# ScalarE takes the bounded drops and the adjacency cast, row maxima and copies are regrouped, and the turns of five engines are redrawn

## The chip, the cores and the metric

The kernel runs on one core of one Trainium2 chip. The metric is device time in microseconds (us) from start to end of one launch; lower is better. The core has four compute engines that run their own instruction streams in program order and meet by semaphores: TensorE (PE, with weight loads shown apart as PEld), VectorE (DVE), ScalarE (ACT) and GpSimd (POOL); SyncE (SP) issues the DMAs.

## The reference

`x` is 16 graphs of 512 nodes with 128 features, `adj` 16 adjacency matrices of 512 x 512. Eight residual blocks follow one another, each on a layer norm of `x`, and no graph needs another:

```python
def reference(x, adj, ...):
    x = x + _L0_gnn_ref(_layernorm(x), adj, ...)   # g0: 3 steps of messages and a GRU cell
    x = x + _L0_ffn_ref(_layernorm(x), ...)        # f0: 8 experts, top 2
    x = x + _L1_gnn_ref(_layernorm(x), adj, ...)   # g1: graph attention, masked softmax, elu
    x = x + _L1_ffn_ref(_layernorm(x), ...)        # f1: attention over 64 slices, 8 heads
    x = x + _L2_gnn_ref(_layernorm(x), adj, ...)   # g2: mean of neighbours, relu
    x = x + _L2_ffn_ref(_layernorm(x), ...)        # f2: Mamba2 block, chunks of 128
    x = x + _L3_gnn_ref(_layernorm(x), adj, ...)   # g3: two layers of 4-head masked attention
    x = x + _L3_ffn_ref(_layernorm(x), ...)        # f3: feed-forward on the top half of the rows
    return x
# in f2, the state stage:
#   Lmat = exp(segsum(dA)): exp of A_cum[l] - A_cum[s] where s <= l, 0 elsewhere
#   Y_diag = einsum('bcln,bcsn,bhcls,bcshp->bclhp', Cc, Bc, Lmat, xdt)
# in g1 and g3: softmax over neighbours, exp(score - row maximum)
```

## The kernel before, in words

Each graph goes through an early half (g0, f0, g1, f1) and a late half (g2, f2, g3, f3). The kernel has 17 half-steps: half-step h runs the early half of graph h and, interleaved with it on every engine, the late half of graph h-1. Half-step 0 has only early work, half-step 16 only late work, and the 15 between have both; they are called periods here. Two sets of tiles (lane 0 and 1) alternate.

What each engine does is written as two Python generators, one for the early and one for the late half, each `yield` being the end of a step. The function `halves` draws steps from the two by a string of letters: `e` is one early step, `l` one late step, `p` a step of the next graph's preparation. For TensorE a digit or `w` issues two small bf16 products of a constant identity into a PSUM bank (`keep_bank`, L1060, tile `ident_bf`, and `keep`, L1056): nobody reads them. Called keeps here, they stand where TensorE would otherwise wait. The strings PE_FIRST, DVE_FIRST and so on hold for half-step 0, PE_TURNS, ACT_TURNS, DVE_TURNS, POOL_TURNS and SP_TURNS for the 15 periods, PE_LAST for half-step 16. So the order on an engine is written out by hand, and every wait is a semaphore between steps. Early TensorE work uses PSUM banks 0 to 2, late work banks 3 to 7.

The steps that the change and the prediction touch:

- g2: `g2_adjacency` casts the int32 adjacency (128 x 2048) to fp32 for the message products, on GpSimd, once per graph (L2082).
- f2: TensorE projects and convolves (`f2_gate`, L444), transposes by constant products (`f2_turn`, L756), then `f2_rows` (TensorE, L794) lays the row copies of the cumulated decays into banks 4, 5, 6 and 3, 4 heads x 128 columns each. VectorE's `f2_rows` (L1362, 16 instructions of 128 x 128) forms min(row - column, 0), ScalarE's `f2_decays` takes exp of it in two pieces of 128 x 1024, and VectorE's `f2_weigh` (L1359) multiplies them into the weights that TensorE uses for Y_diag.
- g1: VectorE's `g1_scores` gives masked scores and one maximum per row tile, `g1_max` finishes all four maxima, ScalarE's `g1_leaky` runs 4 times and `g1_exp` 4 times, TensorE turns the result.
- g3: per layer 16 blocks (4 row tiles x 4 heads), each masked (DVE L1860), exponentiated (ACT), normalised (POOL L2089) and transposed by TensorE (`g3_turn`, L903). The transposed block is copied out of PSUM by `g3_turned`: every fourth one by VectorE (L1877), the other three by ScalarE (L1068, tiles adjf and scratch).
- f1: `to_columns` (L453) transposes the normalised rows, then projections, slice softmax, `f1_mix` and `f1_out`, whose end releases the next graph's first product.

Of the kernel before, what the change touches and what calls it, by code (L numbers as in the profile page):

```python
# [20 lines left out]
ALU = mybir.AluOpType  # L21
# [3 lines left out]
P = 128  # L25
# [52 lines left out]
    "lleele"  # L78
)
PE_FIRST = (  # L80
    "eewwwwwweeeeeeeeeewwwwwwwwwwwwwwwwwwwwwwwwwwwwwwwwweeeeeeeeeewwwwwwwwwwwwwwwwwwwwwwwwwwwwwwwwweeeeee"
    "eeeewwwwwwwwwwwwwwwwwwwwwwwwwwwwwwwwweppeeeewwwwwwwwweeeeeeeeeeeeeeeeeeeeeeeeeeeeeeeeeeeeeeeeeeeewww"
    "wwwwwwwweeeeewwwwwwwwwwwwwwwwwwwwwwwwwwwwwwwwwwweeeewwwwwweeewwwwwwwwwwwwwwwwwwwwwwwwwwwwwwwwwwweeww"
    "wwwwwewwwwwewwwwwweeeewwwwwwwwwwwwwwwwwwwwwwwwwwwwwwwwwwweeeewwwwwwewwwwewwwwwwwwwwwwwwwwwwweewwwwwe"
    "wwwwwwwwwwwwwwwwwwwwwwewwwwwwweeeeewwwwwwwwwwwwwwwwwwwwwwwwewwwwwwwewwwwwweewwwwwwwwwwwwewwwwwwewwww"
    "wweeee"
# [3 lines left out]
    "wwwwwwwwwlllwwlwlllllllwwwwwwwwwwwwwwwwwwwwwwwwwwwwwwwwwwwlllllllwwwlwwwwwwwwwwwwwwwwwwwwwwwwwllllww"  # L90
    "wwwwwwwwwwwwwwwwwwwwwwwwwwwwwwwwwllllwwwwwwllllwwwwwwwwwwwwwlwwwwwwwwwwwwwwwwwwwwwwwwwwwwllwwwwwwwww"
    "lwwwwwwwwwwwwlllwwwwwwwlwwwwwwwwlwwwwwwwwwwwwlllwwwwwwllllwwwwlwwwwwwwwlwwwwwwwwwwwwllwwwlwwwwwllwwl"
    "wwwwwwllllwllllwwwwwwwwwwwwwlwwwwwwwwwwwwwwwwwwwwwwwwwwwwllwwwwwwwwwlwwwwwwwwwwwwlllwwwwwwwlwwwwwwww"
    "lwwwwwwwwwwwwlllwwwwwwllllwwwwlwwwwwwwwlwwwwwwwwwwwwllwwwlwwwwwllwwlwwwwwwllllwwwllllwwwwwwwwwwwwwww"
    "wwwwwwwwwwwwwwwwwwwwllllwwwwwwllllwwwwwwwl"
# [8 lines left out]
    "ee7777eelellll7777lllllleeeeeeellll7777lllleleeleeeeeellell7lllllll11eeeeeeeeellellll77l7l7777777777"  # L104
    "7e777777777777lllleeee777777eee777777777lleelleelllleeleeee7777leeelleeeeellleleele33333llllllleeeel"
    "eeeeleeeeeeeeeeell44eellelleellll33lleleeeleee7l7777777777777777777eele77e777777leeeel1111lll11111l1"
    "1111111111l11eeeelellellllel111111lellel44ll4lelllleeeeelllle77777e77777ellllelellelelllelee"
)
ACT_TURNS = (
    "eellleeelellllllleellllleleelellleeeeleeeeeelleelllleelllllllllllllleeelelleeleelllllllleleeeeeeelee"  # L110
    "eelleellllllelllllelllelelelellllllelelleleeeeleellll"
)
DVE_TURNS = (
# [2101 lines left out]
```

## Time and profile before

| | |
|---|---|
| time, median of 3 runs | 3431.71 us (3428.83 to 3431.92) |
| the profiled execution | 3433.32 us, of it the span 3431.5 us |
| TensorE clock granted, mean | 0.994 of full |
| PE busy | 3231.9 us, 94% |
| DVE busy | 2208.7 us, 64% |
| ACT busy | 1752.7 us, 51% |
| POOL busy | 693.3 us, 20% |

The busy share says how long an engine had an instruction in flight. For TensorE it includes the keeps, so 94% is not 94% of needed work. The 17 half-steps can be told apart in the trace by the transposes of `x_in_ln` (L453), which open each early half.

### The profile page before, as it was taken

What the parts mean: (1) busy time and instruction counts of PE and PEld (TensorE: products, weight loads), DVE (VectorE), ACT (ScalarE), POOL (GpSimd) and SP (SyncE); (2) the same over time, 40 slices, a digit from 0 to 9 for tenths busy, and PEclk for the clock granted to TensorE, in tenths of its full rate; (3) what the DMA queues carried; (4) which work ended last, traced back from release to release, by engine and by line L of the source; (5) the groups of instructions that cost most, each with busy time, mean ns of one, the idle gap of its engine ahead of it and who ended that gap; (6) DMA issues with size and microseconds to landing.
All of it is one profiled execution on the core that took longest, in us unless ns stands there. A gap on an engine that the chain in (4) does not pass through costs nothing.

```text
span 3431.5 us, 62674 instructions
## 1 busy us (share of the span) xinstructions
PE 3231.9 (94%) x24744; PEld 2268.1 (66%) x24776; DVE 2208.7 (64%) x7062; ACT 1752.7 (51%) x3195; POOL 693.3 (20%) x804
## 2 busy tenths in 40 slices
PE   8999999999999999999999999999999999999989
PEld 5766666666666666666666666666666666666677
DVE  3476666757567676666757567676666757566653
ACT  2237454563645537454563645537454563645524
POOL 0012122121221212122121221212122121221212
PEclk9999999999999999999999999999999999999999
DMA  3000000000000000000000000000000000000000
GB/s 132 2 7 1 20 4 17 7 1 20 4 17 7 1 22 1 19 4 17 7 1 19 4 17 7 1 22 1 19 4 17 7 1 19 1 4 4 1 8 5
DMA packets 28773, 40.68 MB, mean 12 GB/s; under 512 B 1344, under 2 KB 17728, under 8 KB 28224
## 3 DMA queue, kind: packets, MB, share of 16 engines
q1 hardware_dynamic: 28480, 36.67, 3.4%
q8 instruction: 197, 3.23, 0.4%
q14 instruction: 96, 0.79, 0.1%
HBM read 28.28 MB, written 4.19 MB: 9 GB/s over the span
## 4 chain that ended last, share of the span: by engine, by line
PE 56%; DVE 26%; ACT 11%; issue 5%; POOL 2%; DVEq 0%
PE ps L444 45%; ACT scratch L1068 8%; DVE scratch L1359 5%; PE ps L903 4%; DVE scratch L1362 4%; DVE scratch L1365 3%; DVE scratch L1860 3%; PE ps L453 2%; DVE x L1365 2%; PE ps L1056 2%; DVE stats L1380 2%; POOL rstd L2066 1%; ACT adjf L1068 1%; DVE xn L1362 1%; ACT xT L1068 1%
## 5 line engine op out<-in xcount | busy, mean ns | idle before, releaser
L1068 ACT ACTIVATE scratch<-scratch 128x512 f32<-128x512 f32 (+4 forms) x832 | 564.8, 691 | 278.9 <-DVE scratch L1359 128.9
L444 PE MATMUL ps<-xT,weights_sb 128*128 128x512 f32 x1152 | 560.9, 604 | 7.9 <-ACT xT L1068 7.8
L444 PE MATMUL ps<-scratch 128*128 128x128 f32 (+6 forms) x4608 | 534.4, 379 | 35.7 <-ACT adjf L1068 14.1
L2089 POOL TENSOR_SCALAR scratch<-scratch 128x512 f32<-128x512 f32 x512 | 352.6, 703 | 933.0 <-DVE scratch L1867 932.3
L1068 ACT ACTIVATE scratch<-ps 128x512 f32<-128x512 f32 (+2 forms) x512 | 286.5, 566 | 426.2 <-PE ps L444 230.7
L444 PE MATMUL ps<-weights_sb,scratch 128*128 128x128 f32 (+3 forms) x3840 | 492.6, 278 | 5.9 <-DVE scratch L1503 5.9
L444 PEld LDWEIGHTS ps<-weights_sb,scratch 128*128 128x128 f32 (+3 forms) x3840 | 442.2, 184 | 56.8 <-issue 29.2
L444 PEld LDWEIGHTS ps<-scratch 128*128 128x128 f32 (+5 forms) x4608 | 341.4, 159 | 174.2 <-issue 92.1
L903 PE MATMUL ps<-weights_sb,scratch 128*128 128x128 f32 x2048 | 307.0, 279 | 61.4 <-ACT adjf L1068 24.6
L2066 POOL TENSOR_TENSOR rstd<-ve,minus_half 128x4 f32<-128x4 f32 x126 | 142.9, 1134 | 1081.0 <-DVE ve L1362 1081.0
L1860 DVE CUSTOM_DVE_ANT_0 scratch<-ps,nomask 128x512 f32<-128x512 f32 x512 | 332.7, 683 | 10.5 <-PE ps L444 10.2
L444 PEld LDWEIGHTS ps<-xT,weights_sb 128*128 128x128 f32 x1152 | 197.9, 190 | 212.8 <-issue 145.0
L903 PEld LDWEIGHTS ps<-weights_sb,scratch 128*128 128x128 f32 x2048 | 222.3, 141 | 170.9 <-issue 104.2
L1060 PE MATMUL ps<-ident_bf 128*128 128x128 bf16 x4140 | 300.4, 219 | 0.0
L1068 ACT ACTIVATE scratch<-ps,weights_sb 128x512 f32<-128x512 f32 x368 | 244.8, 686 | 88.5 <-PE ps L444 87.7
L1060 PEld LDWEIGHTS ps<-ident_bf 128*128 128x128 bf16 x4140 | 264.4, 99 | 34.1 <-issue 29.4
L1068 ACT ACTIVATE scratch<-ps,made_sb 128x512 f32<-128x512 f32 x176 | 120.4, 684 | 301.2 <-PE ps L444 301.0
L1068 ACT ACT_TABLE_LOAD x202 | 259.2, 1283 | 18.2 <-PEq L252 14.7
L1068 ACT ACTIVATE xT<-ps 128x512 f32<-128x512 f32 x112 | 66.9, 597 | 342.4 <-PE ps L453 342.4
L444 PE MATMUL ps<-adjf,scratch 128*32 128x256 f32 (+1 forms) x1280 | 241.6, 425 | 0.0
L1365 DVE SCALAR_TENSOR_TENSOR x<-ps,scratch,x 128x128 f32<-128x128 f32 x576 | 161.8, 344 | 111.5 <-PE ps L444 93.6
L1068 ACT ACTIVATE adjf<-ps 128x512 f32<-128x512 f32 (+1 forms) x288 | 166.3, 577 | 89.5 <-PE ps L903 67.2
(166 smaller groups left out, 4520.1 us busy)
## 6 DMA issues: line engine op xcount, KB each, us to landing
adj<-adj SPq DMA_DIRECT2D x16, 1024.0 KB, 5.7
weights_sb<-weights SPq DMA_DIRECT2D x1, 4605.0 KB, 19.0
x_in<-x SPq DMA_DIRECT2D x16, 256.0 KB, 2.8
scratch<-scratch SPq DMA_DIRECT2D x32, 128.0 KB, 2.3
out<-x SPq DMA_DIRECT2D x16, 256.0 KB, 2.4
scratch<-raw SPq DMA_DIRECT2D x1, 1645.0 KB, 22.4
weights_sb<-weights SPq DMA_DIRECT2D x1, 499.0 KB, 6.5
scratch<-raw SPq DMA_DIRECT2D x1, 384.0 KB, 4.9
```

The source lines that it names most:

```text
L444: return pe.matmul(o, lhsT, rhs, start=start, stop=stop, **k)
L453: last = pe.transpose((ep if k < G2 else lp)(0, P, P, t * P), rows[:, t, 0:D], ident)
L903: last = pe.transpose(lp(turn_bank(n), P, P, j * P), probabilities(g, layer, n)[:, tile(j)], ident)
L1056: pe.matmul(ep(0, P) if h else lp(3, P, P, 384), ident_bf[:, :], ident_bf[:, :], start=True, stop=True)
L1060: pe.matmul(banks[k][0:P, 0:P], ident_bf[:, :], ident_bf[:, :], start=True, stop=True)
L1068: return act.activation(o, a, func, **k)
L1359: return v.tensor_tensor(o, a, c, op)
L1362: return v.tensor_scalar(o, a, s1, s2, op0, op1, **k)
L1365: return v.scalar_tensor_tensor(out=o, in0=a, scalar=s1, in1=c, op0=op0, op1=op1, **k)
L1860: v.tensor_tensor_reduce(probabilities(g, layer, n), lp(n % AH), NM[g][:, n // AH, :], -1.0, 4 * BIG, ALU.add, ALU.min, cut(g, G3_MX + n, ...
L2066: pool.tensor_tensor(rstd[g][:, :], ve[g][:, :], minus_half[:, :], ALU.pow).then_inc(s[f"rstd_ready{g % LANES}"], 1)
L2089: pool.tensor_scalar(p, p, cut(g, G3_RI + n, 1), 1.0, ALU.mult, ALU.mult).then_inc(s["att_p"], 1)
```

## The change

It has these parts.

- The bounded drops of f2 leave VectorE. ScalarE's new `f2_drops` forms relu(column - row) with scale -1 and the column as bias, and `f2_decays` takes exp with scale -1. The second `f2_rows` exp of ScalarE now stands after the third group of drops.
- `g2_adjacency` leaves GpSimd for ScalarE (a Copy of 128 x 2048), and stands after the third `g0_candidate`.
- `g1_max` works on pairs of row tiles, with one semaphore step for each pair, and ScalarE's order is leaky 0, leaky 1, exp 0, leaky 2, exp 1, leaky 3 and so on.
- The copies of g3's transposed blocks are split evenly: even blocks on VectorE (16 per graph, before 8), odd ones on ScalarE (16, before 24).
- All turn strings are redrawn. Per period the keeps go from 276 to 290 products, in half-step 0 from 756 to 750 by its string, in half-step 16 from 1034 to 1074.

```diff
 PE_TURNS = (
-    "ee7777eelellll7777lllllleeeeeeellll7777lllleleeleeeeeellell7lllllll11eeeeeeeeellellll77l7l7777777777"
+    "ee7777eeeeelelleleleelllllleeeeeeellll7777llllell7777777777777777777777777777777leellllllllleleeeeel"
...
@@ semaphores @@
-            "... "m1_ready": 1, ...
+            "... "m1_ready": T // 2, ...
-            "... "pT_dve": 2 * T, "pT_act": 2 * T * (AH - 1), ...
+            "... "pT_dve": T * AH, "pT_act": T * AH, ...
         def turned(layer, n, g):
-            if n % AH == 0:
-                return done("pT_dve", g, layer * T + n // AH)
-            return done("pT_act", g, (layer * T + n // AH) * (AH - 1) + n % AH - 1)
+            return done("pT_act" if n % 2 else "pT_dve", g, (layer * T * AH + n) // 2)
@@ ScalarE @@
+                def g2_adjacency(g):
+                    yield
+                    act.wait_ge(*done("aggr_psum", g, GNN0_STEPS - 1))
+                    f(AF[g][:, :, :], ADJ[g][:, :, :], ACT.Copy).then_inc(s["adjf_ready"], 1)
@@
-                    if t == 0:
-                        act.wait_ge(*done("m1_ready", g))
+                    if t % 2 == 0:
+                        act.wait_ge(*done("m1_ready", g, t // 2))
@@
+                def f2_drops(g):
+                    for n, c in enumerate((1, 2, 3, 0)):
+                        yield
+                        act.wait_ge(*done("row_psum", g, n))
+                        for h in range(MH):
+                            a = F2_S + 9 * 16 + c * MH + h
+                            last = f(cut(g, F2_E + (c * MH + h) * P, P), lp(c, P, P, h * P), ACT.Relu, scale=-1.0, bias=SC[g][:, a:a + 1])
+                        last.then_inc(s["dd_ready"], 1)
+                        if n == 2:
+                            yield from f2_rows(g, 1)
@@ f2_decays
-                        f(e, e, ACT.Exp).then_inc(s["e_ready"], 1)
+                        f(e, e, ACT.Exp, scale=-1.0).then_inc(s["e_ready"], 1)
@@ g3 on ScalarE
-                            if n > AH and n % AH:
+                            if n > AH and n % 2:
                                 yield from g3_turned(g, layer, n - AH)
@@ VectorE
-                def f2_rows(g):
-                    for n, c in enumerate((1, 2, 3, 0)):
-                        yield
-                        v.wait_ge(*done("row_psum", g, n))
-                        for h in range(MH):
-                            a = F2_S + 9 * 16 + c * MH + h
-                            last = ts(cut(g, F2_E + (c * MH + h) * P, P), lp(c, P, P, h * P), SC[g][:, a:a + 1], ALU.subtract, 0.0, ALU.min)
-                        last.then_inc(s["dd_ready"], 1)
@@
+                            if q:
+                                yield from g3_turned(g, layer, (q - 1) * AH + 2)
@@ GpSimd
-                def g2_adjacency(g):
-                    yield
-                    pool.wait_ge(*done("aggr_psum", g, GNN0_STEPS - 1))
-                    pool.tensor_copy(AF[g][:, :, :], ADJ[g][:, :, :]).then_inc(s["adjf_ready"], 1)
```

How the instructions stand in a row, at the places of which the prediction speaks. Names: ps0 to ps7 are PSUM banks; in the rows of one period here scratch1, xT1 and adjf1 (or those with 0) belong to one graph and the other number to the other.

ScalarE around the decays of f2 (late graph 0, early graph 1), before:

```order
955 L1068 ACTIVATE scratch1<-ps0,made_sb 128x512
956 L1068 ACTIVATE scratch1<-scratch1,weights_sb 128x512
957 L1068 ACTIVATE adjf0<-ps7 128x512
958 L1068 ACTIVATE scratch1<-ps1 128x512
959 L1068 ACTIVATE adjf0<-ps7 128x256
960 L1068 ACTIVATE scratch0<-scratch0 128x1024 x2
961 L1068 ACTIVATE scratch1<-ps0,made_sb 128x512
```

and with the change:

```order
905 L1066 ACTIVATE scratch1<-ps0,made_sb 128x512
906 L1066 ACTIVATE scratch1<-scratch1,weights_sb 128x512
907 L1066 ACTIVATE adjf0<-ps7 128x512
908 L1066 ACTIVATE scratch0<-ps4,scratch0 128x128 x4
909 L1066 ACTIVATE scratch0<-ps5,scratch0 128x128 x4
910 L1066 ACTIVATE scratch0<-ps6,scratch0 128x128 x4
911 L1066 ACTIVATE adjf0<-ps7 128x256
912 L1066 ACTIVATE scratch0<-ps3,scratch0 128x128 x4
913 L1066 ACTIVATE scratch1<-ps1 128x512
914 L1066 ACTIVATE scratch0<-scratch0 128x1024 x2
```

The 16 drops stand between the two exponentials of the rows, and the early graph's copy (scratch1 from ps1) stands behind all of them.

VectorE at the same place, before:

```order
1820 L1359 TENSOR_TENSOR scratch1<-xT1,scratch1 128x512
1821 L1365 SCALAR_TENSOR_TENSOR scratch1<-scratch1 128x512
1822 L1362 TENSOR_SCALAR scratch0<-ps4,scratch0 128x128 x4
1823 L1365 SCALAR_TENSOR_TENSOR xT1<-scratch1 128x512
1824 L1362 TENSOR_SCALAR scratch0<-ps5,scratch0 128x128 x4
1825 L1362 TENSOR_SCALAR scratch0<-ps6,scratch0 128x128 x4
1826 L1362 TENSOR_SCALAR scratch0<-ps3,scratch0 128x128 x4
1827 L1359 TENSOR_TENSOR scratch0<-adjf0,scratch0 128x768
1828 L1359 TENSOR_TENSOR scratch0<-scratch0 128x768
1829 L1414 COPY scratch1<-ps1 128x512
1830 L1359 TENSOR_TENSOR scratch0<-scratch0 128x1024 x2
```

and with the change:

```order
1862 L1776 COPY scratch0<-ps6 128x512
1863 L1379 TENSOR_TENSOR scratch1<-xT1,scratch1 128x512
1864 L1385 SCALAR_TENSOR_TENSOR scratch1<-scratch1 128x512
1865 L1385 SCALAR_TENSOR_TENSOR xT1<-scratch1 128x512
1866 L1379 TENSOR_TENSOR scratch0<-ps3,weights_sb 128x512
1867 L1379 TENSOR_TENSOR scratch0<-adjf0,scratch0 128x768
1868 L1379 TENSOR_TENSOR scratch0<-scratch0 128x768
1869 L1379 TENSOR_TENSOR scratch0<-scratch0 128x1024
1870 L1434 COPY scratch1<-ps1 128x512
1871 L1379 TENSOR_TENSOR scratch0<-scratch0 128x1024
```

The drops are gone, the early graph's new state (xT1) is no longer between them, and its copy from ps1 stands between the two long products.

TensorE after the projections of f2 (`f2_gate`, the products from xT1), before:

```order
516 L444 MATMUL ps5<-xT1,weights_sb 128x512
517 L444 MATMUL ps1<-adjf0,scratch0 128x512 x3
518 L444 MATMUL ps0<-xT0,weights_sb 128x512
519 L444 MATMUL ps2<-scratch0,made_sb 128x512
520 L444 MATMUL ps1<-scratch0,made_sb 128x512
521 L756 MATMUL ps6<-weights_sb,scratch1 128x128 x4
```

and with the change:

```order
517 L442 MATMUL ps5<-xT1,weights_sb 128x512
518 L1058 MATMUL ps7<-ident_bf 128x128 x62
519 L754 MATMUL ps6<-weights_sb,scratch1 128x128 x4
520 L442 MATMUL ps1<-scratch0,made_sb 128x512
521 L442 MATMUL ps0<-scratch0,made_sb 128x512
522 L754 MATMUL ps4<-weights_sb,scratch1 128x128 x4
```

Between the last projection and the first transpose stood early message and gate products; they now come before the projections, and 62 keeps stand there.

TensorE at the end of a period, from the slice softmax of f1 to the next graph's first transpose, before:

```order
479 L671 MATMUL ps1<-weights_sb,scratch1 64x128 x4
480 L949 MATMUL ps5<-weights_sb,scratch0 128x128 x4
481 L444 MATMUL ps3<-xT0,weights_sb 128x512
482 L444 MATMUL ps0<-scratch1 64x128 x8
483 L444 MATMUL ps4<-xT0,weights_sb 128x512
484 L444 MATMUL ps1<-scratch1 128x128 x4
485 L444 MATMUL ps6<-weights_sb,scratch0 128x128 x12
486 L444 MATMUL ps1<-scratch1 128x128 x4
487 L444 MATMUL ps6<-weights_sb,scratch0 128x128 x4
488 L444 MATMUL ps1<-scratch1 128x128 x8
489 L453 MATMUL ps0<-weights_sb,x_in_ln0 128x128 x4
```

and with the change:

```order
481 L442 MATMUL ps0<-scratch1 64x64 x8
482 L442 MATMUL ps6<-weights_sb,scratch0 128x128 x12
483 L669 MATMUL ps1<-weights_sb,scratch1 64x128 x4
484 L1058 MATMUL ps7<-ident_bf 128x128 x10
485 L442 MATMUL ps0<-scratch1 64x128 x8
486 L442 MATMUL ps6<-weights_sb,scratch0 128x128 x4
487 L442 MATMUL ps1<-scratch1 128x128 x16
488 L451 MATMUL ps0<-weights_sb,x_in_ln0 128x128 x4
```

The late graph's f3 (ps3, ps4, ps6) has moved ahead, and f1's last products (ps1) stand together behind it.

## Rows read from the trace of the kernel before

**Rows 1.** The page: span, and busy time of each engine.

```profile
span 3431.5 us, 62674 instructions
PE 3231.9 (94%) x24744; PEld 2268.1 (66%) x24776; DVE 2208.7 (64%) x7062; ACT 1752.7 (51%) x3195; POOL 693.3 (20%) x804
```

**Rows 2.** Windows of one period in three stretches, and of half-step 16; columns named.

```profile
core 0: us, PE busy (x) PEld busy (x) DVE busy (x) ACT busy (x) POOL busy (x), PEclk, DMA share, GB/s
...
1001.57:1067.19 65.62, 62.75 (x382) 40.27 (x383) 51.23 (x136) 27.21 (x40) 8.58 (x6) 1.00 0.11 29
1067.19:1125.80 58.61, 55.50 (x414) 38.45 (x412) 32.75 (x116) 41.52 (x73) 12.96 (x18) 1.00 0.00 1
1125.80:1207.34 81.54, 76.48 (x658) 56.23 (x657) 53.20 (x190) 41.16 (x87) 21.90 (x26) 1.00 0.00 1
...
3264.00:3431.50 167.50, 151.19 (x1710) 123.36 (x1708) 78.97 (x265) 62.86 (x126) 29.88 (x40) 0.96 0.02 6
```

**Rows 3.** The same three stretches, keeps alone (tile ident_bf: PE, PEld, DVE busy).

```profile
1001.57:1067.19 65.62, 6.05 (x82) 5.46 (x82) 0.00 (x0) 1.00 0.11 29
1067.19:1125.80 58.61, 3.72 (x52) 3.38 (x52) 0.00 (x0) 1.00 0.00 1
1125.80:1207.34 81.54, 10.26 (x142) 8.79 (x142) 0.00 (x0) 1.00 0.00 1
```

**Rows 4.** Timeline of PE: f1's first transpose and the next graph's, half-step 0, then period.

```profile
137.94 1.10 PE L453 MATMUL ps<-weights_sb,xn 128*128 128x128 f32 x4 [2.87 <-DVE xn L1362]
...
177.79 0.60 PE L453 MATMUL ps<-weights_sb,x_in_ln 128*128 128x128 f32 x4
...
1156.51 1.09 PE L453 MATMUL ps<-weights_sb,xn 128*128 128x128 f32 x4 [0.33 <-DVE xn L1362]
...
1207.34 0.66 PE L453 MATMUL ps<-weights_sb,x_in_ln 128*128 128x128 f32 x4 [0.17 <-DVE x L1365]
```

**Rows 5.** Chain that ended last, a piece of f2 in this period.

```profile
1050.42 2.58 DVE scratch L1359 x2
```

**Rows 6.** DVE by form, f2_weigh's long products: period 1001.57 on, then half-step 16.

```profile
L1359 DVE TENSOR_TENSOR scratch<-scratch 128x1024 f32<-128x1024 f32 x2 | 4.3, 2208 | 0.0
...
L1359 DVE TENSOR_TENSOR scratch<-scratch 128x1024 f32<-128x1024 f32 x2 | 2.4, 1222 | 0.0
```

**Rows 7.** Timeline of POOL at the same place of the period.

```profile
1049.63 1.94 POOL L2082 CAST adjf<-adj 128x2048 f32<-128x2048 int32 x1 [30.05 <-PE ps L444]
1051.53 2.06 POOL L2070 TENSOR_TENSOR x<-x,weights_sb 128x512 f32<-128x512 f32 x1
```

**Rows 8.** Timeline of DVE in half-step 16: the 16 drops.

```profile
3304.92 4.22 DVE L1362 TENSOR_SCALAR scratch<-ps,scratch 128x128 f32<-128x128 f32 x16 [2.26 <-PE ps L794]
```

**Rows 9.** Timelines of ACT: short and long instructions of its kinds.

```profile
1046.83 2.00 ACT L1068 ACTIVATE scratch<-scratch 128x1024 f32<-128x1024 f32 x2 [1.51 <-DVE scratch L1362]
...
1107.24 0.38 ACT L1068 ACTIVATE scratch<-ps 128x256 f32<-128x256 f32 x1
1107.51 0.69 ACT L1068 ACTIVATE scratch<-ps,weights_sb 128x512 f32<-128x512 f32 x1
...
3291.08 0.22 ACT L1068 ACTIVATE scratch<-scratch 128x16 f32<-128x16 f32 x1
```

**Rows 10.** g3's copies: DVE by form in the period, ACT in its timeline.

```profile
L1877 DVE COPY scratch<-ps 128x512 f32<-128x512 f32 x8 | 5.5, 690 | 9.7 <-PE ps L903 9.7
...
1099.80 0.57 ACT L1068 ACTIVATE adjf<-ps 128x512 f32<-128x512 f32 x1
```

**Rows 11.** PE's waits in the period: in total, times, longest.

```profile
PE ps L903 <- ACT adjf L1068: 1.6, 5, 0.4
PE ps L903 <- DVE scratch L1877: 1.4, 3, 0.9
```

**Rows 12.** Timelines at g1: ACT's rectifiers with the first exp, DVE's end of g1_max.

```profile
1135.54 3.16 ACT L1068 ACTIVATE scratch<-scratch 128x512 f32<-128x512 f32 x5
...
1137.35 0.16 DVE L1365 SCALAR_TENSOR_TENSOR scratch<-scratch 128x4 f32<-128x4 f32 x1
```

**Rows 13.** Timeline of PE in half-step 16: one long run of keeps.

```profile
3277.35 4.07 PE L1056 MATMUL ps<-ident_bf 128*128 128x128 bf16 x70
```

More of the change, by code:

```diff
@@ L908, in g3_values @@
                     yield
-                    pe.wait_ge(*turned(layer, AH * (2 * pair + 1), g))
+                    pe.wait_ge(*turned(layer, AH * (2 * pair + 2) - 2, g))
                     pe.wait_ge(*turned(layer, AH * (2 * pair + 2) - 1, g))
@@ L1223, in f2_log, with f2_rows @@
                     f(cut(g, F2_S + 3 * 16, 16), cut(g, F2_S + 2 * 16, 16), ACT.Ln).then_inc(s["dt_act"], 1)
-                def f2_rows(g):
-                    for n, width in enumerate((2 * MI, MI)):
-                        yield
-                        act.wait_ge(*done("gt_re_psum", g, 1 + n))
-                        f(AF[g][:, n, 0:width], lp(4, width), ACT.Exp).then_inc(s["re_ready"], 1)
+                def f2_rows(g, n):
+                    width = (2 * MI, MI)[n]
+                    yield
+                    act.wait_ge(*done("gt_re_psum", g, 1 + n))
+                    f(AF[g][:, n, 0:width], lp(4, width), ACT.Exp).then_inc(s["re_ready"], 1)
+                def f2_drops(g):
+                    for n, c in enumerate((1, 2, 3, 0)):
+                        yield
+                        act.wait_ge(*done("row_psum", g, n))
[5 more added lines that the diff above has]
+                            yield from f2_rows(g, 1)
                 def f2_decays(g):
@@ L1283, in g0 @@
                         yield from g0_candidate(g, k)
+                    yield from g2_adjacency(g)
                 def f0(g):
@@ L1294, in g1 @@
                     yield from g1_project(g)
-                    for t in range(T):
-                        yield from g1_leaky(g, t)
+                    yield from g1_leaky(g, 0)
+                    yield from g1_leaky(g, 1)
                     for t in range(T + 1):
@@ L1299, in g1 @@
                             yield from g1_exp(g, t)
+                        if t < 2:
+                            yield from g1_leaky(g, t + 2)
                         if t >= 1:
@@ L1324, in f2 @@
                     yield from f2_log(g)
-                    yield from f2_rows(g)
+                    yield from f2_rows(g, 0)
+                    yield from f2_drops(g)
                     yield from f2_decays(g)
@@ L1539, in g1_scores, with g1_max @@
                                            ALU.add, ALU.min, cut(g, G1_MX + t, 1)).then_inc(s["u1_ready"], 1)
-                def g1_max(g):
-                    mx = cut(g, G1_MX, T)
+                def g1_max(g, q):
+                    mx = cut(g, G1_MX + 2 * q, 2)
                     yield
-                    v.wait_ge(*done("u1_ready", g, T - 1))
-                    own(tt(mx, mx, cut(g, G1_F, T), ALU.subtract))
+                    v.wait_ge(*done("u1_ready", g, 2 * q + 1))
+                    own(tt(mx, mx, cut(g, G1_F + 2 * q, 2), ALU.subtract))
                     own.wait()
@@ L1956, in g1 @@
                         yield from g1_scores(g, t)
-                    yield from g1_max(g)
+                        if t % 2:
+                            yield from g1_max(g, t // 2)
                     yield from g1_end(g)
@@ L1984, in f2 @@
                     yield from f2_turn(g)
-                    yield from f2_rows(g)
                     yield from f2_reading(g)
```

54 lines of the change are left out of this document (26 added, 28 removed).

## The prediction

> **What bounds the kernel now.** I read the busy shares first [rows 1]: TensorE 94%, the others 20 to 64%. Then the windows of one of the 15 periods, cut in three at products easy to find in the trace: A (f2 beside g0), B (g3's first layer beside f0), C (g3's second layer and f3 beside g1 and f1) [rows 2], and the keeps alone in the same windows [rows 3]. A to C add up to 205.77 us. TensorE is busy for 62.75 + 55.50 + 76.48 = 194.73 us of it, but 6.05 + 3.72 + 10.26 = 20.03 us are keeps, which stand in for waiting. So needed work is 174.7 us, and 11.0 us idle plus 20.0 us keeps, 31.0 us in all, is time in which TensorE has nothing it may do: A 8.9, B 6.8, C 15.3 us. The change alters no needed product of TensorE. What it can gain or lose is part of these 31 us. Where they come from is a dependence, seen in the chain of waits: in A it runs on VectorE and ScalarE through f2; in C it is f1's own row of small steps. f1 from its first transpose to the next graph's takes 177.79 - 137.94 = 39.9 us when nothing lies beside it, and 1207.34 - 1156.51 = 50.8 us in a period [rows 4].
>
> **Drops (f2).** They cost VectorE 4.22 us for 16 [rows 8], and this leaves it. On ScalarE no row has this form. Bounds: 0.22 us as for 128 x 16, 0.38 as for 128 x 256 from PSUM, which is followed 0.27 us later by the next instruction [rows 9]. I take 0.28, near that distance: 16 x 0.28 = 4.5 us, bounds 3.5 and 6.1. The exponential has to wait for all of them either way, and they start on the same row products; so on the path of f2 they are worth +0.3 us (-0.7 to +1.9). VectorE no longer delays the drops by the early graph's state (xT1, one 128 x 512 instruction, which at 0.69 us a copy of that width [rows 10] covers the 0.3): 0. VectorE gets 4.2 us back off the path.
>
> The Trainium skill (ScalarE: Activation LUTs, Rules for kernel authors) says the opposite of this part: a relu belongs on VectorE, since an ACTIVATE costs about 0.3 us fixed and 0.83 ns an element. An estimate from that page is 0.41 us for 128 columns and 6.5 us for 16, a little beyond my upper bound; rows 9 have 128 x 16 done in 0.22 us, less than the page's fixed part, so I keep to the row. By the page f2 would be 2 us later than in my sum, and rival 2 near its deciding point.
>
> **Adjacency cast.** GpSimd's cast takes 1.94 us, its bias addition then 2.06 [rows 7], and just there VectorE's two long products of f2 take 2208 ns each; in half-step 16, with no graph beside it, the same two take 1222 ns [rows 6]. They are on the chain that ended last, with 2.58 us for the piece [rows 5]. With the cast on ScalarE and the addition issued right behind the layer norm, nothing of GpSimd lies there: 2 x (2208 - 1222) = 2.0 us off the late chain in A. On ScalarE the cast costs about what two exponentials of 128 x 1024 do, 2.0 us [rows 9], behind the last g0 candidate, where it holds up only later copies (bounds 1.9, GpSimd's own time, and twice it, since no row of ScalarE has an integer input).
>
> The skill (SBUF: State Buffer, the section on two separate sides) calls this an exclusive lock between VectorE and GpSimd, held for a whole instruction, and names a VectorE instruction with two SBUF inputs against a GpSimd one that reads SBUF. Rows 6 and 7 agree. By that rule the addition, moved earlier, may block another VectorE instruction instead and give 1 us of the 2 back.
>
> **Copies of g3.** VectorE takes 8 more, ScalarE 8 fewer: 8 x 0.69 = +5.5 us of VectorE, 8 x 0.57 = -4.6 us of ScalarE [rows 10]. With 4.5 for the drops and 2.0 for the cast ScalarE gains 1.9 us of work a period, on 109.9 of 205.8; VectorE has +5.5 - 4.2 - 2.0 = -0.7. Neither comes near the bound. TensorE waits 1.6 us for ScalarE's and 1.4 us for VectorE's copies [rows 11]. An even split takes some of the first and adds to the second: 3.0 us to be had at most, I take 0.5, of it 0.3 in B and 0.2 in C.
>
> **Row maxima of g1.** All four rectifiers and the first exp take 3.16 us from 1135.54, and the maxima are done at 1137.51 [rows 12]. By pairs, the first exp can begin after two rectifiers, about 2 x 0.6 = 1.2 us sooner. TensorE's first turn comes as much sooner, and g1 heads the chain through f1 in C: up to -1.2, if the rest of g1 isn't held by g3 on the same engines. I take -0.4.
>
> **Turns.** Keeps: 70 in 4.07 us [rows 13], 0.058 us each. Counted from the order, A has 122 instead of 82 (+2.3 us), B 44 instead of 52 (-0.5), C 124 instead of 142 (-1.0). In A, early products that stood between f2's projections and its transposes now come first, and 62 keeps (3.6 us) stand there. f2's projections start later by those products and its transposes about when they did; the keeps fill the hole, so A's sum of keeps and idle goes up by 2.3 less what idle the keeps replace (2.87 us there is in A, 65.62 - 62.75 [rows 2]). In C, f1's last steps stand behind f3 instead of between its products, so f1 no longer waits for 16 transposed products and a 128 x 512 one between its last 16; of the 50.8 - 39.9 = 10.9 us that company costs f1, I take 0.5.
>
> **The sum of a period.** A: -2.0 (contention) + 2.3 (keeps) - 0.3 (idle they replace) = 0, between -0.9 and +0.7. In B and C a keep taken away pays only as far as the wait that it filled gets shorter, so keeps and waits are not added. B: the copies 0.3 and late work drawn closer behind f0's 0.3, about what the keeps lose (0.5): -0.6, between -2.0 and +0.5. C: maxima 0.4, copies 0.2, f1's tail 0.5, about what its keeps lose (1.0): -1.1, between -5, half of the 10.9, and +1.7, all keeps kept in time and ScalarE's surplus on the path. Together -1.7 us, times 15 = -25.5. Half-step 0: 6 keeps fewer and g1 by pairs, -0.3. Half-step 16: 40 keeps more, 2.3 us if each costs; most stand behind shorter waits, and the contention is absent there already, so +0.8 (-1 to +2.3). Total -25.0. Against the profiled execution's own 3433.3 us (span 3431.5) this gives 3408.3; that execution lies 1.6 above the median of the runs shown, so **3407 us**.
>
> **Rivals.**
> 1. No change within 0.2% (6.9 us, about what a measurement of this kernel can tell from no change). PE's needed work stays, the chain moves from VectorE to ScalarE with 0 gained, and the 2.0 us of contention are used up by A's 2.3 us of keeps; B and C only shift waits. For it: 94% busy, and 14 more keeps a period. Time 3425 to 3438, say 3431. Chance 0.14.
> 2. Slower. ScalarE runs in program order: its copy of the early state (from ps1, ahead of the exponentials) now stands behind 16 drops, which wait for TensorE's last row product. If that copy comes 2 us late, g0's next step and TensorE's products behind it are late, while nothing fills the gap but what the string gives. Also 1.9 us more on ScalarE. It decides from 2.2 us a period, 1.7 for my gain and 0.46 for the 6.9 us of the bound (15 x 0.46); at 2.9 us, a net of +1.2, it gives 3450. Against it: ScalarE is busy for 27 of A's 65.6 us [rows 2], and the copy itself is short. Chance 0.22.
> 3. Much faster. C's walk of f1 comes near its time alone: -5 us there, -6 in all, 15 x 6 = 90, 3342; halfway 3380. For it: C holds half of the 31 us. Against: VectorE and ScalarE are busy for 53 and 41 of its 81.5 us, with g3's steps between. Chance 0.12.
> 4. The forecast, some 0.3 to 1.3% faster. Chance 0.52.
>
> **Range and chances.** Per period the unknowns together are about -4.0 to +0.6: 3432 - 60 = 3372 below, 3432 + 9 = 3441 above, which leaves part of rival 3 below and part of rival 2 above. Range 3372 to 3441; the forecast's own is 3388 to 3422. Faster 0.64 (0.52 + 0.12), same 0.14, slower 0.22.
>
> **What the changed profile would show.** Right: the two long f2 products at about 1.22 us each in a period, and GpSimd without a cast; 16 ScalarE drops in 4 to 5 us, the exponential following at once; ScalarE at some 52% busy, VectorE at 64%; windows of a period adding up to about 204 us, A unchanged, C shorter by 1 us; TensorE's needed work at 174.7 us still. Wrong: drops over 0.35 us each; TensorE idle for ScalarE's copy from ps1 in A; f2's first transpose waiting behind the 62 keeps' end, or its inputs ready long before they end, so that the keeps themselves are the delay; the copies' waits on VectorE above 3 us. The forecast is wrong if A grows by more than B and C give, or if C gives several times what I took.

## The result, and the profile after

The changed kernel takes 3333.60 us (median of 4 runs, 3332.15 to 3336.56) against 3431.64 before: ratio 0.9717, 95% interval 0.9700 to 0.9734, so 98 us or 2.8% faster. The forecast was 3407, with 3372 as the low end of its range. The profiled execution took 3333.91 us, its span is 3332.1 us.

The page of the changed kernel, span and busy times as in [rows 1]:

```profile
span 3332.1 us, 63179 instructions
PE 3189.0 (96%) x25003; PEld 2274.5 (68%) x25020; DVE 2206.0 (66%) x6966; ACT 1787.1 (54%) x3341; POOL 629.6 (19%) x788
```

One period is 1170.88 - 972.02 = 198.9 us long instead of 205.8. For the comparison the border between B and C must be a point that both orders have, and my border of [rows 2] was none. From here on B ends at g1's first transposes (L453, L451 after). Before, in windows of the period that [rows 2] show (PE, PEld, DVE, ACT, POOL busy, clock):

```profile
1067.19:1129.92 62.73, 59.46 (x427) 40.25 (x426) 34.69 (x126) 41.90 (x74) 13.98 (x19) 1.00 0.00 1
1129.92:1207.34 77.42, 72.53 (x643) 54.42 (x644) 51.26 (x179) 40.78 (x86) 20.88 (x25) 1.00 0.01 1
```

After, the windows A, B, C and half-step 16:

```profile
972.02:1037.59 65.57, 62.67 (x424) 42.27 (x423) 46.07 (x123) 31.84 (x56) 4.86 (x5) 1.00 0.10 29
1037.59:1093.77 56.18, 54.55 (x407) 37.51 (x405) 36.77 (x130) 39.55 (x69) 13.83 (x19) 1.00 0.01 1
1093.77:1170.88 77.11, 74.39 (x641) 55.43 (x639) 54.05 (x183) 40.53 (x84) 20.66 (x25) 1.00 0.01 1
3159.60:3332.10 172.50, 156.13 (x1743) 127.10 (x1742) 78.79 (x252) 61.00 (x133) 29.76 (x40) 0.93 0.02 6
```

The reader is to see three things. A is unchanged at 65.6 us. B and C together go from 140.15 to 133.29 us, all of the gain. Part of what B lost went to C: the new order moves eight products of 128 x 512 of g3's second layer from B to C, about 3.5 us, so on equal terms B is some 3 us shorter and C some 4. And half-step 16, counted from its first transposes (g2's) to the end, took 168.2 us in this profile where it took 162.4 before; how much of that is the change is seen below.

TensorE's time in a period splits as follows. It is worked out from all rows of the timeline of PE of each period: each row's time up to the next start, less the idle time noted there. "waits" is how many idle times are noted.

```
            length  needed  keeps  idle  waits
before       205.8   175.1   20.4  10.3     34
after        198.9   172.6   19.9   6.3     21
```

The same by stretch, with C cut once more at f1's first transposes; "rest" is keeps and idle time together:

```
                            length  needed   rest
A                 before      65.6    56.8    8.8
                  after       65.6    55.0   10.5
B                 before      62.7    55.3    7.4
                  after       56.2    51.8    4.3
C up to f1        before      26.6    17.2    9.4
                  after       32.9    24.8    8.1
C from f1 on      before      50.8    45.7    5.2
                  after       44.2    40.9    3.3
```

So the gain in B and C is 6.2 us of keeps and idle time (3.1 in B, 3.1 in C) and 0.7 us of the needed column. f1's own stretch is 6.6 us shorter, but 4.8 us of this is needed work: late products that stood in it now stand ahead of it.

The waits of TensorE in B and C together, after, that answer to [rows 11] (total, times, longest):

```profile
PE ps L901 <- ACT adjf L1066: 0.5, 2, 0.3
PE ps L901 <- DVE scratch L1888: 0.5, 2, 0.3
PE ps L901 <- POOL scratch L2097: 0.4, 2, 0.2
```

They were 1.6 and 1.4 us. The chain that ended last tells the same from its side. By engine, before and then after:

```profile
PE 56%; DVE 26%; ACT 11%; issue 5%; POOL 2%; DVEq 0%
```

```profile
PE 73%; DVE 14%; ACT 9%; issue 3%; POOL 1%; DVEq 0%
```

More of it runs on TensorE itself, and half as much on VectorE. The "needed" products took 2.5 us less, 1.8 of it in A, although they are the same ones. A reading that was not traced through: short delays between neighbours are merged into the rows of the view and count as work. f1's four first transposes show one such case. They are one row of 1.09 us before [rows 4] and one of 0.60 us after.

### The profile page after: what moved, and what is told of

Its sections match the earlier page's. It is cut to its first block, busy times and chain, and to the rows that moved or that the text cites. A ratio compares the mean times of both kernels' runs of the same rounds, so it can differ in the third digit from the quotient of the medians.

```text
span 3332.1 us, 63179 instructions
## 1 busy us (share of the span) xinstructions
PE 3189.0 (96%) x25003; PEld 2274.5 (68%) x25020; DVE 2206.0 (66%) x6966; ACT 1787.1 (54%) x3341; POOL 629.6 (19%) x788
## 4 chain that ended last, share of the span: by engine, by line
PE 73%; DVE 14%; ACT 9%; issue 3%; POOL 1%; DVEq 0%
PE ps L442 59%; ACT scratch L1066 6%; PE ps L901 6%; DVE scratch L1385 4%; DVE scratch L1379 3%; PE ps L451 2%; PE ps L1054 2%; DVE scratch L1888 1%; DVE scratch L1871 1%; POOL scratch L2097 1%; DVE scratch L1382 1%; ACT adjf L1066 1%; PE ps L614 1%; ACT xT L1066 1%; DVE x L1385 1%
## 5 line engine op out<-in xcount | busy, mean ns | idle before, releaser
L442 PE MATMUL ps<-xT,weights_sb 128*128 128x512 f32 x1152 | 568.4, 603 | 7.3 <-ACT xT L1066 7.2
L442 PE MATMUL ps<-scratch 128*128 128x128 f32 (+6 forms) x4608 | 526.7, 378 | 26.0 <-ACT adjf L1066 6.6
L1066 ACT ACTIVATE scratch<-ps 128x512 f32<-128x512 f32 (+2 forms) x384 | 212.2, 561 | 325.8 <-PE ps L442 212.2
L2080 POOL TENSOR_TENSOR rstd<-ve,minus_half 128x4 f32<-128x4 f32 x126 | 128.7, 1021 | 1223.6 <-DVE ve L1382 1222.0
L1058 PE MATMUL ps<-ident_bf 128*128 128x128 bf16 x4350 | 310.1, 219 | 0.0
L1888 DVE COPY scratch<-ps 128x512 f32<-128x512 f32 x256 | 175.4, 685 | 147.4 <-PE ps L901 145.8
```

Of the source, the lines that this page charges most:

```text
L442: return pe.matmul(o, lhsT, rhs, start=start, stop=stop, **k)
L1058: pe.matmul(banks[k][0:P, 0:P], ident_bf[:, :], ident_bf[:, :], start=True, stop=True)
L1066: return act.activation(o, a, func, **k)
L1888: v.tensor_copy(pt[:, :, tile(n // AH % 2)], lp(turn_bank(n)).rearrange("p (j n) -> p j n", j=T)).then_inc(s["pT_dve"], 1)
L2080: pool.tensor_tensor(rstd[g][:, :], ve[g][:, :], minus_half[:, :], ALU.pow).then_inc(s[f"rstd_ready{g % LANES}"], 1)
```

## Experiments

The four reassignments (drops, cast, maxima, copies of g3) and the order are taken apart. A "fall" is a stretch in which the granted clock of TensorE was at its lower level (1.2 GHz); the stretch lengths given are of periods without one, unless it is said. "Old order" and "new order" are the turn strings of the kernels before and after on all engines, with the steps of the other assignment set in where they fit. Time is the median; the kernel before was 3432 to 3434 us beside these runs.

**All reassignments back, new order.** The edits to the functions are those of the diff, reversed; in the strings the steps moved.

> The changed kernel's order on every engine, but all four reassignments taken back: drops on VectorE right behind its copy of f2_turn, cast on GpSimd behind the bias addition, one copy in four of g3 on VectorE, g1's maxima at once. Theory O (the order alone makes the gain, by fewer waits of TensorE, 34 a period before and 21 after): 3335 to 3360 us. Theory R (the reassignments make it): above 3400 us. Theory J (they need each other): 3380 us or more, and the run with the old order and the reassignments above 3410 too.

3412.6 us, ratio 0.9939 (0.9921 to 0.9956). The new order alone gives 0.6%. Theory O falls; the time lies where Theories R and J both have it, and the next run decides between them. In a period without a fall A is 67.1, B 57.8 and C 78.0 us, 2.9 us less than before in all; ten of the 15 periods had a fall that cost 1.9 us (last section).

**All reassignments, old order.**

> The kernel before with all four reassignments, in the old order of turns (the moved steps are set in where they fit). Theory O: 3415 to 3445 us, the contention of 2.0 us a period gone, at most 20 us gained. Theory R: 3335 to 3360 us. Theory J: 3410 us or more.

3531.3 us, ratio 1.0282 (1.0266 to 1.0298): 2.8% slower than before. A fell to 64.1 us (1.5 of the 2.0 us that I had reckoned for the contention), B rose to 66.4 and C to 80.8. Theories O and R fall, Theory J (they need each other) stands, and my rival that ended on the slow side came true for this order, though in B and C and not in A.

**Copies split as before, new order.**

```diff
-            return done("pT_act" if n % 2 else "pT_dve", g, (layer * T * AH + n) // 2)
+            if n % AH == 0:
+                return done("pT_dve", g, layer * T + n // AH)
+            return done("pT_act", g, (layer * T + n // AH) * (AH - 1) + n % AH - 1)
```

> The changed kernel with g3's copies split as before (VectorE every fourth, ScalarE three of four). Theory O: within 10 us of 3334. Theory C (the even split carries the gain of stretch B, where 6.5 us a period went): 3334 + 15 x 3 to 15 x 6.5, so 3380 to 3430 us, with half-step 16 about 2 us shorter in either case, since it grew by 2.4 us from g3 on.

3360.2 us, 26.6 us more than the changed kernel: a period is about 1.8 us longer (B 1.6, C 0.2). In the new order the split is worth 1.8 us a period, not 3 to 6.5 and not 0. Half-step 16 was expected 2 us shorter; it took 167.5 us from its first transposes, 0.7 less.

**Drops back on VectorE, new order.**

The functions are those of before; VectorE's call stands here:

```diff
+                    yield from f2_rows(g)
                     yield from f2_reading(g)
```

> The changed kernel with the drops back on VectorE, right behind f2_turn's copy. Theory O and my sum (drops even on the path): within 8 us of 3334. Theory D (they clear VectorE for the early half): 3350 to 3380 us. Half-step 16 from f2's transposes to g3's should be 2 to 2.5 us shorter than the changed kernel's 49.2 us, if the drops on ScalarE are what lengthened it.

3335.3 us, the same as the changed kernel. A period is 0.3 us longer. Theory D falls. In half-step 16 the stretch from f2's transposes to g3's is 47.8 instead of 49.2 us, but this doesn't show that the drops lengthened it: with the drops on ScalarE the same stretch took 47.9 us in the run with the maxima at once and 48.1 in the one with the cast back, whose half-step 16 is the changed kernel's.

**Cast back on GpSimd, new order.**

> The changed kernel with the adjacency cast back on GpSimd, behind the bias addition. If the cast beside VectorE's long products is what costs (2.0 us by the rows of before; A is 1.5 us longer with all reassignments taken back): 3334 + 15 x 1.5 = 3357 us, and the two products at about 2200 ns again. If the lateness lies elsewhere in the taken-back parts: 3334 to 3340 us.

3332.7 us, the same. One of the two long products of f2 was slowed by the cast, as its mean shows beside the changed kernel's (first the changed kernel, then this one; DVE by form):

```profile
L1379 DVE TENSOR_TENSOR scratch<-scratch 128x1024 f32<-128x1024 f32 x2 | 2.4, 1221 | 0.0
```

```profile
L1373 DVE TENSOR_TENSOR scratch<-scratch 128x1024 f32<-128x1024 f32 x2 | 3.5, 1766 | 0.0
```

The slowed one lies over the cast, which ran from 1022.61 to 1024.68 (its row stands further below), and ended 1.08 us behind it. Timeline of DVE in the same run:

```profile
1023.45 2.31 DVE L1373 TENSOR_TENSOR scratch<-scratch 128x1024 f32<-128x1024 f32 x1
```

Their sum is 1.1 us longer, and the period is 199.0 us. In the new order VectorE's f2 products have that much room. With all four reassignments taken back A was 67.1 us (first run), 1.5 more than after. Of the four only drops and cast lie in A, so each alone costs nothing or 0.3 us and both together about 1.5; a run with just these two back was not made.

**Maxima at once, new order.**

> The changed kernel with g1's maxima finished at once and the four rectifiers ahead of the first exp. My sum gave them 0.4 us a period, bounds 0 and 1.2: 3340 us, between 3334 and 3352. If keeps fill the hole and the later copies catch up: 3334 us.

3343.4 us, 9.8 more: 0.7 us a period in the stretch from g1's to f1's first transposes (33.6 instead of 32.9). The pairs are worth 0.65 us a period where I reckoned 0.4.

**Old order in one stretch.** All engines' strings are cut at two points where old and new order have done the same steps: at f0's and at g1's first transposes on TensorE, and at the matching places of the others.

> All four reassignments; the old order on every engine up to f0's first transposes (stretch A), the new order from there to the period's end. The old order with the reassignments had A in 64.1 us, the new one 65.6. Theory S (the stretches are independent): 3334 - 15 x 1.5 = 3312 us. Theory L (the new A hands on the late half in a better state, and the 62 keeps buy it): B grows by what A gives, 3330 us or more.

3319.6 us, ratio 0.9670 (0.9656 to 0.9685). A is 64.7 us, 0.9 shorter and not 1.5, and B and C are as in the changed kernel. So the stretches are independent as Theory S said, with less to win in A than its 3312 us took. This is faster than both kernels.

> All four reassignments; the old order only in stretch B (f0 beside g3's first layer), new order before and behind it. Theory B (the gain and the loss of the reassignments in the old order sit in B's order): B 66 us instead of 56 but less of the rest, 3334 + 15 x 6 to 15 x 10, so 3424 to 3484 us. Theory C (the gain is in f1's stretch, where f1 is 6.6 us shorter): within 20 us of 3334.

3457.3 us. B is 63.3 us, C 77.4: B's order carries 7.3 us a period, 7.1 of it in B. About the rest of the 124 us are falls, in 11 of the 15 periods, which cost 1.5 us each.

> All four reassignments; the old order only in stretch C (g3's second layer and f3 beside g1 and f1). In the old order with the reassignments this stretch took 29.0 + 51.8 = 80.8 us against 77.1 in the new one. Theory B: 3334 + 15 x 0 to 15 x 3.7, so 3334 to 3390 us. Theory C: 3390 us or more.

3452.4 us. B is 60.3, C 80.8. C's order carries 7.9 us a period: C is 3.7 us longer, and B 4.1, of which 3.5 are the eight products of g3 that the old order has in B. Eleven of the 15 periods had a fall. Each of Theories B and C named the right range for its own stretch and took the other stretch for nearly free, so both are too narrow.

**Keeps.** In the string the run of 62 is cut.

```diff
-7777777777777777777777777777777
+777777777777777
```

> The changed kernel with the run of 62 keeps behind f2's projections cut to 30 in each of the 15 periods; nothing else differs. My sum charged 2.3 us a period for A's 40 additional keeps. Theory K (keeps cost what they take): 3334 - 15 x 32 x 0.058 = 3306 us. Theory W (they stand in for a wait on f2's convolution, since TensorE waits 0.41 us behind them anyway): the idle time grows by the 1.85 us that the keeps shrink, 3332 to 3337 us as long as the granted clock stays at full; if it drops in the hole, each dip costs 1.5 to 2 us, up to 3364 us.

3339.2 us (3334.8 to 3344.9), 5.6 us more. Timeline of PE behind f2's projections in this run, in a period that then lost clock:

```profile
999.77 1.84 PE L1058 MATMUL ps<-ident_bf 128*128 128x128 bf16 x30
1003.81 0.63 PE L754 MATMUL ps<-weights_sb,scratch 128*128 128x128 f32 x4 [2.20 <-ACT scratch L1066]
```

Windows of A in that period and in the next; PEclk is the third number from the end:

```profile
969.49:1036.31 66.82, 62.30 (x392) 41.18 (x391) 45.99 (x123) 31.81 (x56) 4.86 (x5) 0.97 0.10 28
1169.60:1235.15 65.55, 60.87 (x392) 40.49 (x391) 46.06 (x123) 31.81 (x56) 4.86 (x5) 1.00 0.10 29
```

The 1.8 us of keeps became 1.8 us of idle time (2.20 instead of 0.41), and A is 65.55 us where the clock held: the same as with 62. In 6 of the 15 periods the clock fell to its lower level (1.2 GHz) for 3.4 us behind that hole, and one fall costs 66.82 - 65.55 = 1.3 us. Theory W stands, the clock included.

**Order against split.** The split was suspected of what the old order loses.

> The old order on every engine with drops, cast and maxima reassigned, g3's copies split as before (one in four on VectorE). Theory P (it is the even split of the copies that the old order can't bear): A 64 us as in the run with all reassignments, B and C as before, so 3432 - 15 x 1.5 = 3409 us. Theory Q (the other three are what hurts in the old order): 3480 us or more.

3410.0 us (ratio 0.9938, 0.9923 to 0.9952), where Theory P said 3409. In the old order the even split alone costs 121 us, and the other three reassignments give 23, all in A (64.1 us; B and C are 62.7 and 77.4 as before).

> The changed kernel with the old order in stretch C and the copies split as before. The even split with this C gave 3452. Theory P: the old C costs only what the order itself is worth, and less than 119 us more than the new C under the same split (3360): 3390 to 3435 us. Theory Q (the old C is bad in itself, whatever the split): 3360 + 119 = 3479 us.

3423.0 us.

> The changed kernel with the old order in stretch B and the copies split as before. With the even split this B took 3457; the run with the old C and the old split says that A and B in the new order give nothing over the old ones under the old split (3410 + 14 for A, against 3423). Theory P: the new B is worth nothing without the even split, so 3360 to 3366 us. Theory Q (the new B is a gain in itself): 3385 us or more.

3420.7 us, at the place of Theory Q. With these the table is complete (us; A new except in the first row):

```
order of B, C      copies as before    copies evenly split
old, old (A old)             3410.0                 3531.3
old B, new C                 3420.7                 3457.3
new B, old C                 3423.0                 3452.4
new B, new C                 3360.2                 3333.6
```

The split costs 121, 37 and 29 us and then gives 27. The first row has the faster A, and some runs have falls, so the clean comparison is B and C together in one period without a fall:

```
order of B, C      copies as before    copies evenly split
old, old                      140.2                  147.2
old B, new C                  138.6                  140.6
new B, old C                  139.3                  141.1
new B, new C                  135.1                  133.3
```

Under the old split the new B alone gives 0.9 us a period, the new C alone 1.6, and both together 5.1. Under the even split they give 6.1, 6.6 and 13.9. So only the new order of both stretches makes the even split pay, and it gives 6.9 us in all, 5.1 from the order and 1.8 from the split. The pairs of maxima stand in every row of this table; without them the order gives 4.3 (B and C are 135.8 us in the first run).

**Why the split costs in the old order.** In the run with the old C and the even split, TensorE waits in B and C chiefly for GpSimd's normalised blocks:

```profile
PE ps L902 <- POOL scratch L2098: 4.7, 5, 2.7
```

GpSimd waits for the reciprocals of VectorE, and these stand in VectorE's queue behind an added copy that waits for TensorE. The timeline of DVE in that run shows one such place:

```profile
1159.12 0.69 DVE L1889 COPY scratch<-ps 128x512 f32<-128x512 f32 x1 [1.10 <-PE ps L902]
1159.73 0.15 DVE L1879 RECIPROCAL scratch<-scratch 128x2 f32<-128x2 f32 x1
```

So the added copy was issued behind the reciprocals.

```diff
-                            if q:
-                                yield from g3_turned(g, layer, (q - 1) * AH + 2)
                             if q < T:
                                 for p in range(2 * q, 2 * q + 2):
                                     yield from g3_sum(g, layer, p)
+                            if q:
+                                yield from g3_turned(g, layer, (q - 1) * AH + 2)
```

> All four reassignments, the old order in stretch C, and VectorE's added copy of g3 (blocks 2, 6, 10, 14) issued behind the two reciprocals of the next row tile instead of ahead of them, in both layers. The same kernel with the copy ahead took 3452, with the copies split as before 3423. Theory V (the added copy waits for its product while reciprocals and f1's reductions stand behind it on VectorE: 4.5 us of such waits in C of that run, and TensorE waits 4.7 us for GpSimd's normalised blocks): the waits for the reciprocals go and the time comes to 3425 to 3440 us. Theory W (the split costs by its number of copies on VectorE, wherever they stand): 3448 us or more.

> The old order everywhere with all four reassignments and the added copy behind the reciprocals. Ahead of them it was 3531, with the copies split as before 3410. Theory V: 3425 to 3480 us, and TensorE's waits for GpSimd's normalised blocks fall from 4.5 us a period to below 2. Theory W: 3520 us or more.

3475.4 us (23 more than with the copy ahead) and 3524.5 us (7 less than 3531.3, which their spreads of 3519.5 to 3529.5 and 3523.5 to 3534.9 can't tell apart). Theory V named 3425 to 3440 and up to 3480, so as a forecast it falls; both times lie in the ranges of Theory W, but its reason, that the place of the copy doesn't matter, does not hold for the first run. What TensorE waits for in the first of these runs, B and C:

```profile
PE ps L902 <- DVE scratch L1889: 6.9, 7, 2.5
PE ps L902 <- POOL scratch L2098: 0.4, 1, 0.4
```

The waits for GpSimd went, as V said (4.7 to 0.4 us), and waits for the copy itself came in their place (0.5 to 6.9 us). So in the old order VectorE brought either the reciprocals or the added copies in time, and neither place got both. That the split loses by exactly this conflict is argued from the waits; no run under the old order removes it.

**A combined version.** A in the old order, all reassignments, and for the last graph alone drops, copies and the string of half-step 16 as before.

> A version to beat both: the old order in stretch A with all reassignments (3319.6 by the earlier run), and for the last graph alone the drops on VectorE, the copies one in four on VectorE and half-step 16's old string of turns. Half-step 16 took 168.2 us from its first transposes in the changed kernel and 162.4 in the one before. Expected 3319.6 - 5.8 = 3314 us; if only the drops count there, 3316.

3319.0 us (ratio 0.9669, 0.9653 to 0.9685), within what can be told from the 3319.6 of the run with the old A. The 3314 us expected were not reached. Half-step 16 was 3.5 us shorter in the profile (164.1 instead of 167.7 us from its first transposes), and half-step 0 was 0.9 us longer. Half-step 0 ends between 172.7 and 179.4 us over the profiles of this study, more than what was to be gained.

**What half-step 16 costs.** Six of the runs have the changed kernel's half-step 16 instruction for instruction (old A, old B, old C, 30 keeps, cast back, maxima at once). From its first transposes it took 164.7 to 167.7 us in their profiles, and 168.2 in the changed kernel's own. The half-step of before took 162.4 us, and 164.1 in the combined version. Two of the identical ones (the changed kernel, then 30 keeps; PEclk is third from the end):

```profile
3163.91:3332.10 168.19, 155.60 (x1738) 126.75 (x1738) 76.29 (x241) 61.00 (x133) 28.74 (x39) 0.94 0.02 5
```

```profile
3167.71:3333.00 165.29, 152.49 (x1738) 124.62 (x1738) 76.32 (x241) 60.96 (x133) 28.69 (x39) 0.97 0.02 5
```

The same 1738 products took 2.9 us more where the granted clock was lower. So the 5.8 us between the two kernels' profiles are in part the clock. The change costs this half-step some 3.5 us on average (166.7 over seven profiles against 163.3 over two).

## Why the prediction was wrong, point by point

**What bounds the kernel.** Right in kind: TensorE's needed products are the same, the room of 31 us was enough, and the gain in B and C came out of keeps and waits. Wrong in one number: "needed work is 174.7 us" took busy time for work. By the same reckoning, busy time less keeps, it is 191.6 - 20.7 = 170.9 us after.

**Drops.** 16 x 0.28 = 4.5 us was nearly right: they took 4.0. Timeline of ACT, after:

```profile
1013.25 3.21 ACT L1066 ACTIVATE scratch<-ps,scratch 128x128 f32<-128x128 f32 x12
1016.26 0.47 ACT L1066 ACTIVATE adjf<-ps 128x256 f32<-128x256 f32 x1
1016.59 1.18 ACT L1066 ACTIVATE scratch<-ps,scratch 128x128 f32<-128x128 f32 x4
```

12 in 3.01 us from start to start, 0.25 each, and 1.02 for the last 4. The estimate of 0.41 from the Trainium skill (ScalarE: Activation LUTs, Rules for kernel authors) is too high here: the trace doesn't agree. Its rule that a relu belongs on VectorE, which the page gives per element and for bf16, decided nothing in a period, where the tiles are fp32 of 128 columns: VectorE's 16 took 4.22 us [rows 8] and ScalarE's 4.0. "Even on the path" holds in the periods (0.3 us). In half-step 16 no cost of theirs is shown beyond the spread.

**Adjacency cast.** The mechanism was right: the two long products take 1221 ns each where they took 2208 [rows 6]. The term, 2.0 us off A by the cast and the addition, was wrong as a term of its own: with the cast alone back on GpSimd nothing is lost. What the traces show is 1.5 us off A for drops and cast together, in the old order (65.6 to 64.1) and in the new one (67.1 to 65.6). How much of it is contention and how much is room on VectorE was not told apart. The Trainium skill's lock (SBUF: State Buffer, the section on two separate sides) is borne out by these rows, and by the product above that ended 1.08 us behind the cast. The addition did not give 1 us back: moved behind the layer norm it takes 1.09 us instead of 2.06 [rows 7]. The timeline of POOL in the run with the cast back on GpSimd shows both:

```profile
995.50 1.09 POOL L2078 TENSOR_TENSOR x<-x,weights_sb 128x512 f32<-128x512 f32 x1 [1.23 <-DVE xn L1376]
...
1022.61 2.07 POOL L2090 CAST adjf<-adj 128x2048 f32<-128x2048 int32 x1 [26.02 <-PE ps L443]
```

**Keeps in A.** "+2.3" was wrong in kind. Half of the 62 keeps gone saves nothing; they filled a hole. The order of A did cost something, 0.9 us with the reassignments (65.6 against 64.7) and 1.5 without (67.1 against 65.6), but not by its keeps. A came out at 0 as forecast, by wrong terms that cancel, which is luck.

**Copies.** Taken at 0.5 us a period, measured 1.8 in the new order and a loss of about 8 us (121 / 15) in the old one. The limit of "3.0 us to be had at most" held for the new order, but my sum had no term for how the split's worth hangs on the order. In the old one the waits point to VectorE's queue, where the added copies and the reciprocals get into each other's way. This step failed.

**Maxima.** Taken at 0.4, measured 0.65.

**Turns in B and C.** This is the step that failed most. I gave B -0.6 and C -1.1, copies and maxima included, and of the order itself only "late work drawn closer" for 0.3 and "f1's tail" for 0.5. B and C gave 6.9 us a period together, four times the 1.7. By the table above, 5.1 of them come from the order under the old split, 1.8 from the split. Two terms were at fault. In B I let "late work drawn closer" pay 0.3, where keeps and idle time fell by 3.1 us. And in C I took 0.5 of the 10.9 us that company costs f1. f1's stretch, from its first transposes to the next graph's, before and then after:

```profile
1156.51:1207.34 50.83, 48.46 (x408) 35.31 (x411) 33.52 (x119) 22.16 (x45) 14.06 (x16) 1.00 0.00 1
```

```profile
1126.67:1170.88 44.21, 43.13 (x353) 32.53 (x353) 31.55 (x108) 18.51 (x33) 12.15 (x13) 1.00 0.00 1
```

It is 6.6 us shorter, with 55 products fewer, some 50 of them products of g3 that now stand ahead of it. So the walk of f1 got shorter chiefly by having less company, and g1, which now shares TensorE with that work and with the projections moved from B, paid for it (26.6 to 32.9 us to f1's first transposes). Keeps and idle time fell by 1.8 us in f1's stretch and by 1.3 in g1's. Rival 3 had f1's walk and 3342 us; I gave it 0.12 because VectorE and ScalarE looked busy, and their busy shares of C (51.3 and 40.8 of 77.4 us, the window above) didn't forbid it. Its number was near, but it put the gain into C, and about half of it is in B. Rival 2's side was real as well, though in B and C and by another queue than I named: the old order with all reassignments is 3531 us.

**Half-step 16.** Taken at +0.8, measured +5.8 us between the two profiles and some +3.5 over all profiles of either version. Which of drops, copies and 40 keeps it is was not shown.

The sum of parts in the new order: copies 26.6, maxima 9.8, drops and cast together about 1.5 x 15 = 22, and 10 x 1.9 = 19 for falls of the run without them (below) make 77 of the 79 us between that run and the changed kernel. The remaining 19 of the 98 us the order gives without any reassignment. Why B and C pay so much more together than alone under the old split was not found.

## What to carry to other kernels

Where the order of several in-order engines is written out by hand, an order and an assignment of work are one choice: price a reassignment under the order that comes with it, since the same split gave 27 us under one and cost 121 under the other. Bound what an order can give by all the time in which the bounding engine does no needed work (here 22.0 us of keeps and idle time in B and C, of which 6.2 went), not by the waits that the trace names for one step (3.0 us), for those say only who came last. Before calling a stretch shorter, count the work in it: most of f1's 6.6 us had only moved. Filler products that stand in a hole cost nothing; count them when asking whether the clock holds, not in the sum.

## What the hardware showed that was not expected

In several runs the granted clock fell to its lower level for 3.4 us at a time (at times 6.8) in the middle of the kernel, where neither the kernel before nor the one after loses any in its periods. Periods with a fall, of 15: 10 with the reassignments taken back, 11 with the old B and 11 with the old C, 6 with 30 keeps, 5 with the old order and all reassignments, 5 with the old B and the old split, and with the copies behind the reciprocals 3 under the old C and all 15 under the old order. For the 30 keeps the hole ahead of the fall is shown above; for the others it was not looked for. Two periods of the first of these runs, one with a fall and one without (windows; PEclk is third from the end):

```profile
579.98:784.75 204.77, 192.71 (x1465) 136.74 (x1465) 137.58 (x440) 110.56 (x200) 41.25 (x50) 0.99 0.03 10
995.27:1198.17 202.90, 191.58 (x1467) 135.24 (x1466) 137.46 (x440) 110.58 (x200) 41.68 (x50) 1.00 0.04 10
```

The same instructions lost the clock in some periods and not in others, and a fall of 3.4 us costs 1.3 to 1.9 us. In half-step 16 the mean granted clock was 0.94 in the changed kernel's profile and 0.97 in the run with 30 keeps, for the same instructions, so its 0.96 before [rows 2] says nothing about the keeps there.
